# Where V of the second half and GpSimd's weight splits stand in a hybrid convolution, attention and expert kernel

## The chip, the core and the metric

The kernel runs on one core of one Trainium2 chip. Its time is the device time of one execution in microseconds. The engines of a core have queues of their own and meet through semaphores: TensorE (PE; its weight loads are PEld), VectorE (DVE), ScalarE (ACT), GpSimd (POOL), and SyncE (SP), which issues most DMAs.

## What is computed

`x` is 4 x 128 x 16 x 16, float32: 1024 tokens of 128 channels. Its three parts follow each other, and each adds to its input.

```python
# 1: convolutional attention over rows; q, k have 16 channels, v 128
x = gamma * einsum('bchk,bhwkv->bcwv', v, softmax(energy)) + x
# 2: tokens t (B, 256, 128), 8 heads of 16
n = layernorm(t)
k, q, v = n @ Wk, n @ Wq, n @ Wv
scores = einsum('bnhd,bmhd->bnmh', k, q) / sqrt(16)
t = t + softmax(scores, axis=-2) @ v
# 3: 8 experts, hidden size 512, the best two by gate logits
n = layernorm(t)
comb = softmax(top 2 of n @ gate_w.T), 0 for the other experts
for e in range(8):
    out += comb[:, e] * (gelu(n @ w1[e].T + b1[e]) @ w2[e].T + b2[e])
t = t + out
```

The reference normalizes each part's tokens as `(n - mean) / sqrt(var + 1e-5)`.

## The kernel before, in words

Channels lie on the partitions, tokens along them. The 1024 tokens are two halves of 512 (four images of 256). The first half goes through convolution and attention; then the expert loop runs over both halves, and the attention of the second half is laid between its steps.

**The expert loop** has 64 steps `n` (`STEPS`): 4 steps of 128 hidden rows for each of 8 experts, for each half (a visit is one expert on one half). `up(n)` makes 128 hidden rows from three passes: w1 and x are each split into a high part and a rest (`w1h`, `w1l`, `x2h`, `x2l`). ScalarE's `gelu(n)` writes `G`. From step 12 on (`SPLIT`, without steps 18 and 22) `G` is also split: a cast makes `Gh` (`high_gelu`, VectorE up to step 23, then ScalarE), a subtraction on VectorE makes `Gl` (`low_gelu`). `down(n)` multiplies with w2, in three passes with `w2h`, `w2l` where `G` is split and in one float32 matmul (two passes in the trace) where it isn't. `LAGS` says how many steps a down-projection lags: at step 12 downs 8, 9 and 10 are issued, at step 16 downs 11 to 14. `weigh(k)` (VectorE) scales a finished visit, `accumulate(k)` (GpSimd) adds it to the output: the first at about step 9, the second at 13.

**w2's split.** ScalarE copies `w2h` of experts 3, 4, 5, 6, 7, 0, 1, 2 (`W2_ORDER`) behind the GELUs of steps 0 to 7. GpSimd's `low_weights2` subtracts to get `w2l`, in the same order, at the places of its own in-order queue that `LOW_W2` gives. GpSimd's queue also holds the gate's exponential (`gate_exp`, at step 2), the pair sums of probabilities (`pair`, at steps 11, 15, 19, 23) and the accumulates. At one step the order is `gate_exp`, `pair`, `low_weights2`, `accumulate`.

**The gate of the first half** runs on VectorE at steps 0 to 4: `top_logits`, `top_experts` (ends with the gap subtraction `g_gap`), GpSimd's `gate_exp`, and `top_weights`, five small operations, each waiting for an earlier one, between the raw maxima (`raw_max`, L682) of steps 2 and 3. TensorE's raw scores (`raw_heads`, L1031) wait for the raw maximum before them.

**The attention of the second half.** Raw scores at steps 2 to 9, `max_transpose` at step 10 and `max_rows` on VectorE, which `scores_of_four(u)` waits for. Units `u` of four heads follow at steps 11, 15, 19 and 23 (`SCORES`): TensorE's scores into banks 4 to 7, two exponentials on ScalarE (`exps`, L503; banks 4 and 5, then 6 and 7), two pair sums on GpSimd. Exponential and GELU need different tables, so each unit has two table loads. On ScalarE `exps` stand ahead of `gelu` of the same step. At step 16 TensorE issues `sums` and `values` of units 4 and 5, behind the downs. V of the second half is projected by `project_v(1)` and copied out by `values_out(1)` (ScalarE, behind the GELU of step `VALUES_AT`).

Of the kernel before, what the change touches and what calls it, by code (L numbers as in the profile page):

```python
# [23 lines left out]
NHALF = T // HALF  # L24
# [14 lines left out]
W2_ORDER = [3, 4, 5, 6, 7, 0, 1, 2]  # L39
# [3 lines left out]
def hybrid_program(nc, x_in, xk_in, convw, convb, bv, gamma, attw, gate, w1, w2, b1, b2, consts, out):  # L43
# [5 lines left out]
    with ExitStack() as ctx:  # L49
# [3 lines left out]
        def sem(name):  # L53
            return ctx.enter_context(nc.semaphore(name))
# [115 lines left out]
        v_done, v_ready, vzero = sem("v_done"), sem("v_ready"), sem("vzero")  # L170
        raw_done, max_ready = sem("raw_done"), sem("max_ready")
        nmT_done, nmT_ready = sem("nmT_done"), sem("nmT_ready")
        score_done, prob_ready, paired, pv_done = sem("score_done"), sem("prob_ready"), sem("paired"), sem("pv_done")
# [13 lines left out]
        part_ready, acc_done, out_sent = sem("part_ready"), sem("acc_done"), sem("out_sent")  # L187
# [27 lines left out]

        FIRST_KQ, SECOND_KQ = (6, 7, 5, 1), ((0, 0), (0, TOK), (1, 0), (1, TOK))
        KQ_BANK = (4, 5, 6, 7)
        V_BANK = [0, 2]
        WARM_BANK = [3, 4, 0, 1]
        U_BANK, Y_BANK, GATE_BANK = (0, 1), (2, 3), (3, 4)  # L220

# [3 lines left out]
        GATING = [0, 32]  # L225
        RAW0, RAW_STEPS, NORM = 2, 8, 27
        SCORES, ATTENDS = {11: 4, 15: 5, 19: 6, 23: 7}, {16: 2, 24: 3}
        LATE_SCORES = (19,)
        HEADS_AT = {0: (2, 3)}
        VALUES_AT = 10  # L230

        G_LOGITS, G_ORDER, G_EXP, G_WEIGHTS, G_ROWS = 0, 1, 2, 2, 4

        SPLIT0, ACT_HIGH = 3 * MT, 24
        SPLIT = [n for n in range(SPLIT0, STEPS) if n not in (18, 22)]
        HIGH_W2 = {n: e for n, e in enumerate(W2_ORDER)}
        LOW_W2 = {n + 1: e for n, e in enumerate(W2_ORDER)}

        def high_engine(n):
            return "dve" if n < ACT_HIGH else "act"  # L240

        def high_count(n):
            return sum(high_engine(k) == high_engine(n) for k in SPLIT if k <= n)

        def split_count(n):
            return sum(k <= n for k in SPLIT)

        def downs(n):

            return range(max(0, n - LAGS[n - 1]) if n else 0, n + 1 - LAGS[n])  # L250

        def part_of(tiles, g, rows, c):

            p = c.start // HALF
            return tiles[p][g][rows, c.start - p * HALF:c.stop - p * HALF]
# [11 lines left out]
        def raw_slot(n):  # L267

            r = n - RAW0
            return (TILES + r // 2, r % 2) if 0 <= r < RAW_STEPS else None  # L270
# [51 lines left out]
        def _(pool):  # L322
# [19 lines left out]
            def low_weights2(e):  # L342

                pool.wait_ge(w2h_ready, W2_ORDER.index(e) + 1)
                if e == W2_ORDER[0]:
                    pool.wait_ge(pv_done, 4)
                    pool.wait_ge(sums_done, 4)
                nc.gpsimd.tensor_tensor(w2l[e][:, :], w2_sb[:, e, :], w2h[e][:, :].bitcast(f32), ALU.subtract)\  # L348
                    .then_inc(w2l_ready, 1)

            def pair(u, s):

                j = slice(2 * s, 2 * s + 2)
                pool.wait_ge(prob_ready, 2 * u + s + 1)
                if u >= 2:
                    pool.wait_ge(sums_done, u - 1)
                nc.gpsimd.tensor_tensor(pairs[:, u % 2, j, :], probs_of(u)[:, j, 0, :], probs_of(u)[:, j, 1, :],  # L357
                                        ALU.add).then_inc(paired, 1)
# [37 lines left out]
            for n in range(STEPS):  # L396
# [5 lines left out]
                if n in SCORES:  # L402
                    for s in range(2):
                        pair(SCORES[n], s)
                if n in LOW_W2:
                    low_weights2(LOW_W2[n])
                for k in range(VISITS - 2):
# [5 lines left out]
        def _(act):  # L413
# [67 lines left out]
            def other_heads(n):  # L481
                act.wait_ge(qkv_done, 8 + n + 1)
                heads_out(n, PS[:, KQ_BANK[n], :], cols(1))

            def values_out(p):

                act.wait_ge(v_done, p + 1)
                act.wait_ge(vzero, 2 * (p + 1))
                dst = vpad[p][:, :, :, :].rearrange("p t h c -> p (t h c)")\
                    .rearrange("p (th r) -> p th r", r=64)  # L490
                src = PS[:, V_BANK[p], :].rearrange("p (th r) -> p th r", r=32)
                for par in range(2):
                    nc.scalar.activation(dst[:, :, 48 * par:48 * par + DK], src[:, :, DK * par:DK * (par + 1)], ACT.Copy)\
                        .then_inc(v_ready, 1)
# [63 lines left out]
            for n in range(STEPS):  # L558
# [4 lines left out]
                for h in HEADS_AT.get(n, ()):  # L563
                    other_heads(h)
                if n == VALUES_AT:
                    values_out(1)
# [282 lines left out]
        def _(pe):  # L849
# [137 lines left out]

            def project_v(p):
                if p:
                    pe.wait_ge(part_ready, 1)  # L990
                else:
                    pe.wait_ge(act_kq_ready, 4)
                for t in range(TILES):
                    last = mm(PS[:, V_BANK[p], t * 128:(t + 1) * 128],
                              xn[:, p * HALF + t * 128:p * HALF + (t + 1) * 128],
                              attw_sb[:, 512:640], start=True, stop=True)
                last.then_inc(v_done, 1)

            def head_rows(j):
                return slice(32 * j, 32 * j + 32)  # L1000
# [77 lines left out]
            def scores_of_four(u):  # L1078

                b, g = u // 2, u % 2  # L1080
                pe.wait_ge(nmT_ready, 6)
                pe.wait_ge(prob_ready, 2 * u)
                if u == 6:
                    pe.wait_ge(t2_ready, 3)
                tok = slice(b * TOK, (b + 1) * TOK)
                for mt in range(2):
                    m = slice(b * TOK + mt * 128, b * TOK + (mt + 1) * 128)
                    for j in range(4):
                        last = mm(PS[:, 4 + j, mt * TOK:(mt + 1) * TOK], part_of(qT, g, head_rows(j), m),
                                  part_of(kT, g, head_rows(j), tok), start=True, stop=True)  # L1090
                        if mt and j % 2:
                            last.then_inc(score_done, 1)
# [72 lines left out]
            def down(n):  # L1165

                k, m = n // MT, n % MT
                e = k % E
                if m == 0:
                    if k in (0, E // 2):  # L1170
                        pe.wait_ge(w2_in[k // (E // 2)], 16)
                    if k >= 2:
                        pe.wait_ge(part_ready, k - 1)
                    if k == 1:
                        pe.wait_ge(combT_ready, 1)
                    if k == 2:
                        pe.wait_ge(v_ready, 2 * NHALF)
                y, ms = PS[:, Y_BANK[k % 2], :], slice(m * 128, (m + 1) * 128)
                if n not in SPLIT:
                    pe.wait_ge(gelu_done, n + 1)  # L1180
                    mm(y, w2_sb[:, e, ms], G[:, n % GR, :], start=(m == 0), stop=(m == MT - 1)).then_inc(down_done, 1)  # L1181
                    return
                if m == 0:
                    pe.wait_ge(w2l_ready, W2_ORDER.index(e) + 1)
                pe.wait_ge(g_high[high_engine(n)], high_count(n))
                mm(y, w2h[e][:, ms], Gh[:, n % GR, :], start=(m == 0), stop=False)  # L1186
                mm(y, w2l[e][:, ms], Gh[:, n % GR, :], start=False, stop=False)  # L1187
                pe.wait_ge(g_low, split_count(n))
                mm(y, w2h[e][:, ms], Gl[:, n % GR, :], start=False, stop=(m == MT - 1)).then_inc(down_done, 1)  # L1189
# [68 lines left out]
            for n in range(STEPS):  # L1258
                if raw_slot(n):
                    raw_heads(*raw_slot(n))  # L1260
                if n in SCORES and n not in LATE_SCORES:
                    scores_of_four(SCORES[n])
                up(n)
                if n in LATE_SCORES:
                    scores_of_four(SCORES[n])
                if n == RAW0 + RAW_STEPS:
                    max_transpose()
                for h in HEADS_AT.get(n, ()):
                    project_other(h)
                if n == VALUES_AT:  # L1270
                    project_v(1)
                for p in range(NHALF):
                    g = n - GATING[p]
                    if g == G_LOGITS:
                        logits(p)
                    if g == G_ROWS:
                        comb_rows(p)
                if n == NORM:
                    norm_center(5)
                if n == NORM + 1:  # L1280
                    norm_var(5)
                for d in downs(n):
                    down(d)
                if n in ATTENDS:
                    for u in (2 * ATTENDS[n], 2 * ATTENDS[n] + 1):
                        sums(u)
                        values(u)
                if n == NORM + 2:
                    norm_spread(5)
            for n in range(STEPS - LAGS[-1], STEPS):  # L1290
                down(n)
# [46 lines left out]
```

## Time and profile before

| | |
|---|---|
| median of 3 runs (lowest, highest) | 186.39 us (186.04, 187.66) |
| the profiled execution: its own time | 186.13 us |
| its span | 184.2 us |
| busy: PE, PEld | 174.1 us (95%), 118.6 us (64%) |
| busy: DVE, ACT, POOL | 117.1 us (64%), 123.2 us (67%), 79.5 us (43%) |
| granted TensorE clock | 1.0 throughout |

The span runs from the first to the last instruction of the profiled execution; its own time includes what lies around the span. Busy times are of that one execution. A line of the timeline gives the start, the duration, the engine, the line of the kernel, what was written from what, how many instructions were merged, and in brackets how long the engine was idle before and what released it. A merged line's duration is that of all its instructions.

### The profile page before, as it was taken

The numbers are of one execution on the slowest core, as the hardware profiler recorded it, in microseconds if no ns is written. First come the engines' busy times: TensorE is split into PE (matmuls) and PEld (weight loads), VectorE is DVE, ScalarE is ACT, GpSimd is POOL, SyncE is SP. The second block draws the span as 40 slices with busy tenths as digits, with TensorE's granted clock in tenths as the row PEclk, the third lists the DMA queues.
The fourth block names the chain that finished last, engine by engine and source line by source line (L and its number), as shares of the span: only waits on it lengthen the run. The fifth ranks groups of instructions, "written<-read, shape, count | busy, mean of one in ns | idle before, by whom it ended". The sixth has DMA issues, their size and how long they took to land.

```text
span 184.2 us, 3336 instructions
## 1 busy us (share of the span) xinstructions
PE 174.1 (95%) x1277; PEld 118.6 (64%) x1277; DVE 117.1 (64%) x199; ACT 123.2 (67%) x185; POOL 79.5 (43%) x68
## 2 busy tenths in 40 slices
PE   6999999989898998999999999999999999999991
PEld 3267867665466544447466567567887888888880
DVE  1569544985465396456084959397888677676673
ACT  3516953317727743545988598867878999999970
POOL 8404228988703284452536093524151152333312
PEclk9999999999999999999999999999999999999999
DMA  5799200000000000570000000000000880000001
GB/s 141 276 374 419 96 0 0 4 0 4 0 5 0 2 0 4 181 271 7 0 0 5 0 0 0 4 0 0 0 7 4 244 269 0 0 4 0 0 0 57
DMA packets 5791, 10.94 MB, mean 59 GB/s; under 512 B 1280, under 2 KB 1664, under 8 KB 5520
## 3 DMA queue, kind: packets, MB, share of 16 engines
q1 hardware_dynamic: 5360, 10.65, 16.7%
q8 instruction: 10, 0.16, 0.3%
q10 hardware_dynamic: 416, 0.08, 0.3%
q14 instruction: 5, 0.04, 0.1%
HBM read 10.17 MB, written 0.56 MB: 58 GB/s over the span
## 4 chain that ended last, share of the span: by engine, by line
PE 73%; issue 8%; ACT 7%; POOL 4%; DVE 4%; DMA 2%; ACTq 0%; DVEq 0%; POOLq 0%
PE PS L1159 9%; PE PS L1163 7%; PE PS L1160 7%; PE PS L1186 6%; PE PS L1189 6%; PE PS L1187 6%; PE PS L1181 4%; POOL pairs L357 4%; PE PS L1017 3%; PE PS L1031 3%; ACT room L516 2%; PE PS L910 2%; PE PS L878 2%; PE PS L1104 2%; DMA convw_sb<-convw 2%
## 5 line engine op out<-in xcount | busy, mean ns | idle before, releaser
L516 ACT ACTIVATE room<-PS,b_sb 128x512 f32<-128x512 f32 x64 | 43.6, 688 | 22.6 <-PE PS L1163 21.2
L772 DVE TENSOR_TENSOR Gl<-room,Gh 128x512 fp32r<-128x512 f32 x50 | 41.2, 831 | 13.7 <-ACT Gh L461 13.0
L365 POOL TENSOR_TENSOR x_sb<-x_sb,room 128x512 f32<-128x512 f32 x15 | 23.6, 1572 | 56.0 <-DVE room L781 56.0
L1159 PE MATMUL PS<-x2h,w1h 128*128 128x512 f32 x64 | 27.4, 427 | 1.2 <-ACT room L516 0.8
L461 ACT ACTIVATE Gh<-room 128x512 fp32r<-128x512 f32 x40 | 25.3, 633 | 1.3
L1163 PE MATMUL PS<-x2l,w1h 128*128 128x512 f32 x64 | 25.5, 398 | 0.0
L1160 PE MATMUL PS<-x2h,w1l 128*128 128x512 f32 x64 | 25.2, 393 | 0.0
L1186 PE MATMUL PS<-Gh,w2h 128*128 128x512 f32 x50 | 20.8, 416 | 0.0
L1187 PE MATMUL PS<-Gh,w2l 128*128 128x512 f32 x50 | 19.8, 395 | 0.0
L1189 PE MATMUL PS<-Gl,w2h 128*128 128x512 f32 x50 | 19.7, 395 | 0.0
L1159 PEld LDWEIGHTS PS<-x2h,w1h 128*128 128x128 f32 x64 | 12.0, 187 | 10.6 <-issue 4.9
L348 POOL TENSOR_TENSOR w2l<-w_sb,w2h 128x512 fp32r<-128x512 f32 x8 | 10.2, 1279 | 12.6 <-ACT w2h L455 12.6
L357 POOL TENSOR_TENSOR pairs<-shared_probs 128x512 f32<-128x512 f32 x10 | 13.7, 1390 | 4.6 <-ACT shared_probs L503 4.6
L1163 PEld LDWEIGHTS PS<-x2l,w1h 128*128 128x128 f32 x64 | 12.0, 188 | 3.5 <-DVE x2l L718 0.6
L682 DVE TENSOR_REDUCE other_nmx<-PS 128x4 f32<-128x1024 f32 x8 | 9.8, 1224 | 6.7 <-PE PS L1031 6.7
L1181 PE MATMUL PS<-room,w_sb 128*128 128x512 f32 x28 | 14.0, 592 | 0.0
L1160 PEld LDWEIGHTS PS<-x2h,w1l 128*128 128x128 f32 x64 | 12.0, 188 | 2.0
L767 DVE CAST Gh<-room 128x512 fp32r<-128x512 f32 x10 | 4.4, 444 | 13.5 <-ACT room L516 13.5
L503 ACT ACTIVATE shared_probs<-PS 128x1024 f32<-128x1024 f32 x12 | 11.6, 1022 | 1.9 <-PE PS L1074 1.7
L781 DVE SCALAR_TENSOR_TENSOR room<-PS,b_sb,room 128x512 f32<-128x512 f32 x16 | 11.9, 744 | 0.7 <-PE PS L1189 0.7
L373 POOL TENSOR_TENSOR ny<-nv,half_power 128x2 f32<-128x2 f32 (+1 forms) x6 | 4.9, 811 | 15.1 <-DVE nv L651 14.4
L1187 PEld LDWEIGHTS PS<-Gh,w2l 128*128 128x128 f32 x50 | 9.4, 188 | 2.6 <-issue 0.5
(136 smaller groups left out, 294.2 us busy)
## 6 DMA issues: line engine op xcount, KB each, us to landing
room<-comb_rows SPq DMA_DIRECT2D x16, 256.0 KB, 5.2
w1raw<-w SPq DMA_DIRECT2D x8, 256.0 KB, 5.9
w_sb<-w SPq DMA_DIRECT2D x2, 1024.0 KB, 10.6
x_sb<-x SPq DMA_DIRECT2D x2, 256.0 KB, 3.2
dev<-xk SPq DMA_DIRECT2D x1, 512.0 KB, 6.3
out<-x_sb SPq DMA_DIRECT2D x2, 256.0 KB, 4.2
attw_sb<-attw SPq DMA_DIRECT2D x1, 320.0 KB, 6.8
cst<-consts SPq DMA_DIRECT2D x1, 228.5 KB, 6.5
```

The lines of the kernel that those rows point to most:

```text
L357: nc.gpsimd.tensor_tensor(pairs[:, u % 2, j, :], probs_of(u)[:, j, 0, :], probs_of(u)[:, j, 1, :], ALU.add).then_inc(paired, 1)
L365: nc.gpsimd.tensor_tensor(t2[:, cols(p)], t2[:, cols(p)], part[:, s, :], ALU.add).then_inc(acc_done, 1)
L461: nc.scalar.activation(Gh[:, n % GR, :], G[:, n % GR, :], ACT.Copy)\
L516: nc.scalar.activation(G[:, n % GR, :], PS[:, U_BANK[n % 2], :], ACT.Gelu, bias=b1_sb[:, c:c + 1])\
L772: nc.vector.tensor_tensor(Gl[:, n % GR, :], G[:, n % GR, :], Gh[:, n % GR, :].bitcast(f32), ALU.subtract)\
L1159: mm(o, w1h[e][:, ms], x2h[:, cols(p)], start=True, stop=False)
L1160: mm(o, w1l[e][:, ms], x2h[:, cols(p)], start=False, stop=False)
L1163: mm(o, w1h[e][:, ms], x2l[:, cols(p)], start=False, stop=True).then_inc(up_done, 1)
L1181: mm(y, w2_sb[:, e, ms], G[:, n % GR, :], start=(m == 0), stop=(m == MT - 1)).then_inc(down_done, 1)
L1186: mm(y, w2h[e][:, ms], Gh[:, n % GR, :], start=(m == 0), stop=False)
L1187: mm(y, w2l[e][:, ms], Gh[:, n % GR, :], start=False, stop=False)
L1189: mm(y, w2h[e][:, ms], Gl[:, n % GR, :], start=False, stop=(m == MT - 1)).then_inc(down_done, 1)
```

## The change

V of the second half is projected at step 12, behind its three downs, into bank 6, and no longer at step 10 into bank 2; it waits for the tenth count of `prob_ready` (both exponentials of unit 4) instead of the first weighing. ScalarE's copies follow GELU 12. The wait for these copies moves from the first down-projection of visit 2 to the scores of unit 5. The up-projection of step 11 is issued ahead of the scores of unit 4 (`LATE_SCORES`). GpSimd's splits of w2 stand at steps 5 to 12 of its queue in place of 1 to 8: behind `gate_exp`, and those of experts 0, 1, 2 behind the first accumulate (step 9), of 1 and 2 also behind the pair sums of unit 4 (step 11).

```diff
-        V_BANK = [0, 2]
+        V_BANK = [0, 6]
...
-        LATE_SCORES = (19,)
+        LATE_SCORES = (11, 19)
         HEADS_AT = {0: (2, 3)}
-        VALUES_AT = 10
+        VALUES_AT = 12
...
-        LOW_W2 = {n + 1: e for n, e in enumerate(W2_ORDER)}
+        LOW_W2 = {n + 5: e for n, e in enumerate(W2_ORDER)}
...
             def project_v(p):
                 if p:
-                    pe.wait_ge(part_ready, 1)
+                    pe.wait_ge(prob_ready, 10)
...
                 pe.wait_ge(nmT_ready, 6)
                 pe.wait_ge(prob_ready, 2 * u)
+                if u == 5:
+                    pe.wait_ge(v_ready, 2 * NHALF)
...
                     if k == 1:
                         pe.wait_ge(combT_ready, 1)
-                    if k == 2:
-                        pe.wait_ge(v_ready, 2 * NHALF)
...
-                if n == VALUES_AT:
-                    project_v(1)
                 for p in range(NHALF):
...
                 for d in downs(n):
                     down(d)
+                if n == VALUES_AT:
+                    project_v(1)
```

## Rows read from the trace of the kernel before

**Rows 1.** The page: the chain by engine (part 4), two groups of VectorE (part 5).

```profile
PE 73%; issue 8%; ACT 7%; POOL 4%; DVE 4%; DMA 2%; ACTq 0%; DVEq 0%; POOLq 0%
...
L767 DVE CAST Gh<-room 128x512 fp32r<-128x512 f32 x10 | 4.4, 444 | 13.5 <-ACT room L516 13.5
...
L781 DVE SCALAR_TENSOR_TENSOR room<-PS,b_sb,room 128x512 f32<-128x512 f32 x16 | 11.9, 744 | 0.7 <-PE PS L1189 0.7
```

**Rows 2.** Timeline of PE and one weight load, 85 to 100 us.

```profile
85.31 1.06 PE L994 MATMUL PS<-attw_sb,xn 128*128 128x128 f32 x8
86.41 1.15 PE L1089 MATMUL PS<-other_kT,other_qT 32*128 32x256 f32 x16
86.41 0.74 PEld L1089 LDWEIGHTS PS<-other_kT,other_qT 32*128 32x128 f32 x16 [0.24 <-DVE other_kT L695]
87.49 0.50 PE L1159 MATMUL PS<-x2h,w1h 128*128 128x512 f32 x1
...
88.98 2.74 PE L1181 MATMUL PS<-room,w_sb 128*128 128x512 f32 x6
92.36 0.50 PE L1159 MATMUL PS<-x2h,w1h 128*128 128x512 f32 x1 [0.64 <-ACT room L516]
...
93.95 1.15 PE L1089 MATMUL PS<-other_kT,other_qT 32*128 32x256 f32 x16
...
99.24 0.40 PE L1189 MATMUL PS<-Gl,w2h 128*128 128x512 f32 x1
```

**Rows 3.** Timeline of ACT, 83 to 95 us.

```profile
83.94 1.38 ACT L516 ACTIVATE room<-PS,b_sb 128x512 f32<-128x512 f32 x2 [1.71 <-PE PS L1163]
86.40 0.66 ACT L493 ACTIVATE other_vpad<-PS 128x256 f32<-128x256 f32 x2 [1.08 <-PE PS L994]
...
88.37 1.94 ACT L503 ACTIVATE shared_probs<-PS 128x1024 f32<-128x1024 f32 x2
90.33 1.28 ACT L516 ACT_TABLE_LOAD   x1
91.62 1.27 ACT L516 ACTIVATE room<-PS,b_sb 128x512 f32<-128x512 f32 x2
93.36 1.39 ACT L516 ACTIVATE room<-PS,b_sb 128x512 f32<-128x512 f32 x2 [0.47 <-PE PS L1163]
```

**Rows 4.** Timelines of POOL, DVE and PE, 63 to 70 us.

```profile
63.37 1.27 POOL L348 TENSOR_TENSOR w2l<-w_sb,w2h 128x512 fp32r<-128x512 f32 x1 [5.60 <-ACT w2h L455]
64.74 1.01 POOL L378 TENSOR_TENSOR g_exp<-euler,g_gap 128x4 f32<-128x4 f32 x1
...
67.35 1.28 POOL L348 TENSOR_TENSOR w2l<-w_sb,w2h 128x512 fp32r<-128x512 f32 x1 [0.36 <-ACT w2h L455]
...
64.00 0.66 DVE L736 TENSOR_TENSOR g_gap<-g_top 128x4 f32<-128x4 f32 x1
...
66.34 0.67 DVE L746 TENSOR_SCALAR g_sum<-g_exp 128x4 f32<-128x4 f32 x1
...
67.42 1.25 DVE L752 TENSOR_TENSOR comb<-g_oh,g_rcp 128x32 f32<-128x32 f32 x1
...
69.87 0.71 PE L1031 MATMUL PS<-other_qT,other_kT 32*128 32x256 f32 x8 [0.58 <-DVE other_nmx L682]
```

**Rows 5.** Timelines of POOL and DVE, 89 to 99 us.

```profile
89.47 2.48 POOL L357 TENSOR_TENSOR pairs<-shared_probs 128x512 f32<-128x512 f32 x2 [3.16 <-ACT shared_probs L503]
94.81 1.41 POOL L365 TENSOR_TENSOR x_sb<-x_sb,room 128x512 f32<-128x512 f32 x1 [2.86 <-DVE room L781]
...
95.10 1.67 DVE L772 TENSOR_TENSOR Gl<-room,Gh 128x512 fp32r<-128x512 f32 x1
...
97.16 1.84 POOL L357 TENSOR_TENSOR pairs<-shared_probs 128x512 f32<-128x512 f32 x1 [0.94 <-ACT shared_probs L503]
```

**Rows 6.** Timelines of POOL and DVE, 123 to 126 us.

```profile
123.32 1.67 POOL L365 TENSOR_TENSOR x_sb<-x_sb,room 128x512 f32<-128x512 f32 x1 [5.80 <-DVE room L781]
...
123.76 1.78 DVE L772 TENSOR_TENSOR Gl<-room,Gh 128x512 fp32r<-128x512 f32 x1
```

## The prediction

> **What bounds the kernel now.** I read the page first, then the timeline of the two stretches that the edits touch, engine by engine. The page's chain [rows 1] gives TensorE 73% of the span and "issue" 8%; TensorE is busy 95% of it. So a time moves only if a TensorE gap closes or opens, and there are two small gaps where the diff works. The first stands at 69.87 us: TensorE is idle 0.58 us ahead of the raw scores of step 4, released by VectorE's raw maximum of step 3 [rows 4]. The second stands at 92.36: 0.64 us ahead of the up-projection of step 13, released by the GELU of step 11 [rows 2]. The reader should see in the ScalarE rows [rows 3] why that GELU is late: GELU of step 10 ends at 85.32, ScalarE waits 1.08 for V, copies V out (0.66), loads the exp table, runs two exponentials (88.37, 1.94 together), loads the GELU table (1.28), and only then computes GELU 11 at 91.62. After the gap everything on TensorE is a chain, each up-projection waiting for a GELU two steps back, so a shift at step 17 is a shift of the end.
>
> **Part 1, V behind the downs of step 12, up-projection 11 ahead of the scores.** Nothing is added: V is the same 8 matmul passes, the same two copies. What moves, on the old time scale:
> The scores of unit 4 still wait for the max rows, whose release came at 86.41 [rows 2] (its weight-load row). Before, V (85.31, 1.06 long) filled the time up to it. Now up-projection 11 does: two ups take 93.95 - 92.36 = 1.59, one 0.80, so 85.31 to 86.11, hidden. Scores start at 86.41 as before.
> The scores end at 86.41 + 1.15 = 87.56. ScalarE started its copy 0.03 after V's end (85.31 + 1.06 = 86.37, then 86.40), so the exponentials can start at 87.59. The table load has no V to wait for: from 85.34 to 86.62, over in time. Before they started at 88.37, so ScalarE gains 0.78. Then exponentials 1.96, table 1.28: GELU 11 starts at 90.84 (91.62 before), its result is there at 91.55, GELU 12 ends at 92.11.
> TensorE: up-projection 12 now stands at 87.49 and takes 0.80: 88.29. Before, two ups stood there, to 88.98. Downs 8, 9, 10 (six passes) took 2.74, less an overlap of about 0.05: 90.98. V costs 0.99 without its overlapped end: 91.97. So up-projection 13 starts at 91.97, not at 92.36: **0.39 gained**, of the 0.64 gap and the 0.78 on ScalarE, because V now lies on TensorE's path where it used to be free. If the cover at 85.31 to 86.41 were not filled, nothing more would be lost, since the scores wait anyway.
> The new waits: V waits for the tenth exponential result (about 89.6), long past. Scores 5, and all that TensorE has queued behind, wait for V's copies: these run after GELU 12, 92.14 to 92.80, and scores 5 come at 93.95 - 0.39 = 93.56. No cost; a slack of 0.76. GELU 13 follows up-projection 13 by 1.00 (92.36 to 93.36), so at 92.97, after the copies. All of the next unit is 0.39 earlier: GELU 14 ends at 94.36, the table is in at 95.64, exponentials 5 start at 95.66.
> The Trainium skill (ScalarE: Activation LUTs, section What ACT_TABLE_LOAD costs) states a drain of about 1.38 us on top of a load of 1.283, for every change of set. In the rows here a load takes 1.28 and the next activation starts 0.01 later (90.33 + 1.28 = 91.61, then 91.62) [rows 3]; by the Trainium skill's sum the load from 85.34 would hold the exponentials to 88.00, and 0.41 of ScalarE's 0.78 would be gone, which still leaves V's end as the last wait. The measurement decides.
>
> **Part 2, GpSimd's splits.** A split is 1.27 to 1.28 us of subtraction over two SBUF inputs, eight of them. GpSimd's queue is in order and not tied to TensorE's steps, so a plan "four steps later" only changes what the splits stand before and after. Three things change: the gate's exponential comes ahead of the first split; splits 0, 1, 2 come behind the first accumulate, which waits for VectorE's weighing at about 85; and splits 1 and 2 come behind the pair sums of unit 4. The down-projections need no split earlier than that of expert 3, at about 96, so no data is late.
> What is late is VectorE. The rows show that a VectorE operation with SBUF inputs doesn't run beside such a GpSimd operation: the gap subtraction on 4 elements took 0.66, from 64.00 to 64.66, against the split of 63.37 to 64.64, and the last gate multiply on 32 elements 1.25, to 68.67, against the split from 67.35 to 68.63 [rows 4]. Gl beside an accumulate (94.81 + 1.41 = 96.22) took 1.67, to 96.77: it finishes 0.55 after the other lets go. And GpSimd waits for VectorE too: a pair sum of 1.24 took 1.84 when Gl had begun first [rows 5].
> Who goes first when both wait? The second Gl at 123.76 was issued behind another Gl and 0.44 after the accumulate of 123.32, and it took 1.78: the accumulate, which had waited, got in between, ended at 124.99, and Gl at 125.54 [rows 6]. So they take turns by order of issue.
>
> *The gate, 64 to 70 us.* The subtraction is no longer held: no row shows it alone, and I take 0.17, between nothing and the 0.44 of a cast on 512 elements [rows 1]; so the gate's exponential starts near 64.25, not 64.74, and ends near 65.26. Then the three first splits, whose inputs are there, follow without a gap: to 66.5, 67.8 and 69.05. VectorE comes out of the first raw maximum at 66.34 with five dependent small operations, four of them on SBUF. Before, the pause of GpSimd up to 67.35 let four of them through and only the last was held. Now the first gets its turn at 66.5, the next (or the next two) at 67.8, the next after 69.05; the last ends at 69.05 + 0.1 to 69.05 + 0.3, against 68.67. Raw maximum and raw scores follow directly. **Cost 0.4 to 0.7, I take 0.6**, nearer to three separate turns, since each operation waits for the one before. The TensorE gap at 69.87 grows from 0.58 to about 1.2. The other end is a gain: if VectorE's small operations all pass, the gap closes, -0.58. Steps 4 to 10 have no slack on TensorE that would take the shift back.
>
> *The splits behind unit 4, 89 to 100 us* (old scale, without that shift). Pair sums started 1.10 after the exponentials (89.47 against 88.37), and two took 2.48: now 88.69 to 91.17. Splits 1 and 2 follow: to 92.44, and to 93.7, or 93.95 if the cast of GELU 12 (issued 92.14, waiting) has its turn between. Gl 12 then ends at 93.95 + 0.55 = 94.5. The weighing, which read PSUM, goes on: 0.74 [rows 1], to 95.15. The accumulate follows at about 95.2 and holds until 96.6 (its 1.41). The cast of GELU 13 lies beside its start (0.44, rows 1). Gl 13 ends at 96.6 + 0.55 = 97.15. Before, it ended at 96.77. Meanwhile exponentials 5 are 0.39 early, so their first pair sum is ready at 95.66 + 1.10 = 96.76, not at 97.16. That is the point: before, the cast and Gl of step 14 were both issued ahead of the pair sum, whose 1.84 shows that it waited for Gl [rows 5]. Now the pair sum is issued at 96.76 and the cast at 97.07. By turns: pair sum to 98.4, cast to 98.7, second pair sum to 99.9, Gl 14 to 100.45. TensorE wants Gl 14 for the last pass of step 14's down-projection at 99.24 - 0.39 = 98.85 [rows 2] and gets it at 100.5. **Cost 1.65, so the stretch ends 1.26 later than before**, the 0.39 of part 1 spent. Sums, attention and step 17 stand behind it on TensorE in one queue. Bounds: if the cast goes first and the pair sum second, Gl 14 ends near 99.3, a stall of 0.45, net nothing; if both go first, net -0.39. I take 1.26 because the issue times are 0.3 apart (0.1 if the cast has no turn between the splits). Here the Trainium skill (SBUF — State Buffer, section Who interferes with whom) says that the operation issued first has the shared ports for its whole length; the row of the second Gl agrees.
>
> **Sum.** 186.13 (the profiled run; span 184.2 and 1.93 around it) + 0.6 + 1.26 = **188.0**. The profiled run lies 0.26 below the median of 186.39.
>
> **Rivals.**
> B: only the gate is late, and step 14's cast slips in before the pair sum. Speaks for it: the margin is 0.1 to 0.35, and a shift of this size in either chain turns it. 186.13 + 0.6 + (0 to -0.39) = 186.3 to 186.7.
> C, the other side, faster: VectorE is held at neither place. The mechanism lies at 66.5: if GpSimd's next split doesn't take the ports as soon as the last one ends, the small gate operations pass in one run, as the four before 67.35 did. It decides once the last gate multiply ends before 68.1, from where the gap of 0.58 is gone, -0.58. With the undisturbed -0.39 of V: 186.13 - 0.97 = 185.2. Against it: the multiply of 67.42 lost to a split by 0.07 already.
> D: the gate costs nothing or gains, the splits behind unit 4 stall step 14: 186.13 + 1.26 + (0 to -0.58) = 186.8 to 187.4.
> E: the change doesn't do what it says, since V on TensorE's path and Gl's delays cancel its gain and the gate comes out level: 186.1.
>
> **How the numbers follow.** Chances: forecast 0.42, B 0.26, C 0.12, D 0.14, E 0.06. The range runs from 185.3 (most of C) to 188.7 (the upper bound of the gate term, 0.7, and some 0.6 of spread between runs). A measurement of this kernel can tell about 1% from no change: that is 184.5 and 188.3 around the median. The forecast lies just inside, so a third to a half of it, and nothing of the rest, is slower by over 1%: 0.20. Faster by over 1% needs more than C gives: 0.03.
>
> **What would show it.** Part 1: up-projection 11 between the max transposes and the scores; GELU 11 some 0.8 earlier after the max rows; no TensorE idle ahead of up-projection 13. Gate: three splits in a row, the last gate multiply's end right after the third, and over 1 us idle ahead of the next raw scores. Unit 4: two splits directly behind two pair sums, Gl 12 over 1 us long, a cast of step 14 over 1 us long, and TensorE idle, released by Gl, ahead of the last pass of step 14. The prediction is wrong if the second is absent (then B or C), or if that Gl is 0.69 long.

## The result, and the profile after

The changed kernel takes 187.57 us (median of 14 runs, 187.45 to 190.89) where the kernel before takes 186.20 (14 runs, 185.98 to 189.05): ratio 1.0082, 95% interval 1.006 to 1.0104. It is 1.37 us slower; 188.0 had been forecast. The highest values of every series here are executions with a lower granted TensorE clock (in the profile of e5 it was 0.83 in the first 20 us and 1.00 after them); a median called "at full clock" below is that of the executions with a mean granted clock of 0.994 or more, and the profiles whose rows are shown have 0.996 or more. The profiled execution after took 187.58, its span is 185.6 against 184.2.

The page after: the chain and the cast, as in [rows 1], the two groups of TensorE that now have idle time ahead of them, and GpSimd's splits:

```profile
PE 70%; issue 9%; DVE 9%; ACT 6%; POOL 4%; ACTq 0%; DVEq 0%; POOLq 0%
...
L1186 PE MATMUL PS<-Gh,w2h 128*128 128x512 f32 x50 | 20.9, 418 | 0.3 <-DVE Gh L767 0.3
L1189 PE MATMUL PS<-Gl,w2h 128*128 128x512 f32 x50 | 19.8, 397 | 1.0 <-DVE Gl L772 1.0
...
L767 DVE CAST Gh<-room 128x512 fp32r<-128x512 f32 x10 | 5.6, 559 | 10.4 <-ACT room L516 10.4
L348 POOL TENSOR_TENSOR w2l<-w_sb,w2h 128x512 fp32r<-128x512 f32 x8 | 10.3, 1302 | 2.9 <-ACT w2h L455 2.9
```

VectorE's share of the chain has gone from 4% to 9%, its mean cast from 444 ns to 559, and TensorE's passes over `Gh` and `Gl` have idle time ahead of them that VectorE releases. No work was added: busy TensorE time is 174.4 us against 174.1.

**The gate.** Timelines after of DVE, POOL (each of the first three splits by itself) and PE, 63 to 71 us, against [rows 4]:

```profile
63.94 0.17 DVE L736 TENSOR_TENSOR g_gap<-g_top 128x4 f32<-128x4 f32 x1
66.27 0.20 DVE L746 TENSOR_SCALAR g_sum<-g_exp 128x4 f32<-128x4 f32 x1
66.38 0.18 DVE L747 TENSOR_TENSOR g_oh<-g_oh,g_exp 128x32 f32<-128x32 f32 x1
66.59 0.18 DVE L749 RECIPROCAL g_rcp<-g_sum 128x4 f32<-128x4 f32 x1
66.69 1.05 DVE L750 TENSOR_TENSOR g_oh<-g_oh 128x32 f32<-128x32 f32 x1
67.78 1.21 DVE L752 TENSOR_TENSOR comb<-g_oh,g_rcp 128x32 f32<-128x32 f32 x1
...
65.16 1.28 POOL L348 TENSOR_TENSOR w2l<-w_sb,w2h 128x512 fp32r<-128x512 f32 x1
66.40 1.30 POOL L348 TENSOR_TENSOR w2l<-w_sb,w2h 128x512 fp32r<-128x512 f32 x1
67.65 1.28 POOL L348 TENSOR_TENSOR w2l<-w_sb,w2h 128x512 fp32r<-128x512 f32 x1
...
70.17 0.71 PE L1031 MATMUL PS<-other_qT,other_kT 32*128 32x256 f32 x8 [0.95 <-DVE other_nmx L682]
```

And one row of the kernel before that [rows 4] lacks, the split between the gate's exponential and the one of 67.35 (timeline, POOL):

```profile
65.71 1.27 POOL L348 TENSOR_TENSOR w2l<-w_sb,w2h 128x512 fp32r<-128x512 f32 x1
```

The gap subtraction takes 0.17, the value I had taken. The splits follow without a pause. Before, two of the five small operations were held: the first (66.34, 0.67 long, to 67.01) until the split of 65.71 was over at 66.98, and the last (1.25). After, the first loses almost nothing (0.20), and two others are held: the fourth (1.05) until the second split is over at 67.70, the fifth (1.21) until the third is, at 68.93. The chain of five takes 2.72 from its first start to its last end, where it took 2.33: 0.39 more. The gap ahead of the raw scores grows from 0.58 to 0.95, so the gate costs 0.37.

**Unit 4.** The timelines after, 85 to 101 us: PE against [rows 2], ACT against [rows 3], POOL and DVE against [rows 5].

```profile
86.73 1.15 PE L1091 MATMUL PS<-other_kT,other_qT 32*128 32x256 f32 x16 [0.24 <-DVE other_kT L695]
88.61 2.73 PE L1181 MATMUL PS<-room,w_sb 128*128 128x512 f32 x6
91.19 1.05 PE L994 MATMUL PS<-attw_sb,xn 128*128 128x128 f32 x8
92.00 0.48 PE L1161 MATMUL PS<-x2h,w1h 128*128 128x512 f32 x1
...
96.15 1.02 PE L1181 MATMUL PS<-room,w_sb 128*128 128x512 f32 x2
98.89 0.50 PE L1186 MATMUL PS<-Gh,w2h 128*128 128x512 f32 x1 [0.33 <-DVE Gh L767]
100.58 0.50 PE L1189 MATMUL PS<-Gl,w2h 128*128 128x512 f32 x1 [0.96 <-DVE Gl L772]
101.00 0.64 PE L1123 MATMUL PS<-pairs,cst 128*32 128x256 f32 x8
...
85.66 1.28 ACT L503 ACT_TABLE_LOAD   x1
87.91 1.94 ACT L503 ACTIVATE shared_probs<-PS 128x1024 f32<-128x1024 f32 x2 [0.97 <-PE PS L1091]
...
91.46 2.70 POOL L348 TENSOR_TENSOR w2l<-w_sb,w2h 128x512 fp32r<-128x512 f32 x2
95.45 1.40 POOL L365 TENSOR_TENSOR x_sb<-x_sb,room 128x512 f32<-128x512 f32 x1 [1.29 <-DVE room L781]
96.81 1.75 POOL L357 TENSOR_TENSOR pairs<-shared_probs 128x512 f32<-128x512 f32 x1
...
93.06 1.65 DVE L772 TENSOR_TENSOR Gl<-room,Gh 128x512 fp32r<-128x512 f32 x1
95.74 1.66 DVE L772 TENSOR_TENSOR Gl<-room,Gh 128x512 fp32r<-128x512 f32 x1
97.32 1.52 DVE L767 CAST Gh<-room 128x512 fp32r<-128x512 f32 x1
98.87 1.65 DVE L772 TENSOR_TENSOR Gl<-room,Gh 128x512 fp32r<-128x512 f32 x1
```

To set the sizes, four more rows of the kernel before (timelines, DVE and PE): the cast and Gl of step 14, the start of step 16's downs and that of the sums behind them:

```profile
96.69 0.42 DVE L767 CAST Gh<-room 128x512 fp32r<-128x512 f32 x1
97.14 0.69 DVE L772 TENSOR_TENSOR Gl<-room,Gh 128x512 fp32r<-128x512 f32 x1
...
96.52 1.02 PE L1181 MATMUL PS<-room,w_sb 128*128 128x512 f32 x2
...
99.56 0.64 PE L1121 MATMUL PS<-pairs,cst 128*32 128x256 f32 x8
```

Before, Gl of step 14 was issued (the start that the timeline gives) at 97.14, 0.02 ahead of the first pair sum of unit 5 (97.16, [rows 5]), and lasted 0.69. After, the pair sum is issued at 96.81, 0.51 ahead of the cast (97.32).

Measured from the scores of unit 4 (86.41 before, 86.73 after), up-projection 13 starts after 5.27 us where it took 5.95, and the downs of step 16 after 9.42 where it was 10.11: 0.69 gained. There is no gap ahead of up-projection 13. The exponentials no longer wait for a table load but for the scores (0.97). From the downs of step 16 to the sums it is 101.00 - 96.15 = 4.85, against 3.04: 1.81 lost. The page's idle figures, 0.33 and 0.96, show only 1.29 of it, for two reasons: a pass that follows an idle stretch has 0.34 to the next start instead of 0.23, and the idle time counts from a modelled end (0.39 after the start) where the next pass would have started after 0.23. The reader should take starts, not idle columns, to size a stall on TensorE.

Together: -0.69 + 1.81 = 1.12 behind the scores. At the gate it is 0.39, since the scores of unit 4 stand 0.32 later though the loop began 0.07 earlier (its first up-projection at 59.19, before 59.26). So 1.12 + 0.39 - 0.07 = 1.44, which is the distance of the two sums (101.00 - 99.56), and the spans differ by 1.4.

### The profile page after: what moved, and what is told of

The parts are those of the page before. It is cut to its first block, busy times and chain, and to the rows that moved or that the text cites. A ratio compares the mean times of both kernels' runs of the same rounds, so it can differ in the third digit from the quotient of the medians.

```text
span 185.6 us, 3336 instructions
## 1 busy us (share of the span) xinstructions
PE 174.4 (94%) x1277; PEld 118.4 (64%) x1277; DVE 120.1 (65%) x199; ACT 123.1 (66%) x185; POOL 79.5 (43%) x68
## 4 chain that ended last, share of the span: by engine, by line
PE 70%; issue 9%; DVE 9%; ACT 6%; POOL 4%; ACTq 0%; DVEq 0%; POOLq 0%
PE PS L1161 8%; PE PS L1165 7%; PE PS L1162 6%; PE PS L1189 6%; PE PS L1186 5%; PE PS L1187 5%; POOL pairs L357 4%; PE PS L1181 3%; PE PS L855 3%; ACT room L516 3%; PE PS L1017 3%; PE PS L1031 2%; PE PS L910 2%; PE PS L878 2%; PE PS L1106 2%
## 5 line engine op out<-in xcount | busy, mean ns | idle before, releaser
L772 DVE TENSOR_TENSOR Gl<-room,Gh 128x512 fp32r<-128x512 f32 x50 | 43.2, 871 | 13.6 <-ACT Gh L461 13.0
L1181 PE MATMUL PS<-room,w_sb 128*128 128x512 f32 x28 | 14.0, 592 | 0.0
L767 DVE CAST Gh<-room 128x512 fp32r<-128x512 f32 x10 | 5.6, 559 | 10.4 <-ACT room L516 10.4
L1189 PEld LDWEIGHTS PS<-Gl,w2h 128*128 128x128 f32 x50 | 9.4, 188 | 3.6 <-DVE Gl L772 1.4
L1186 PEld LDWEIGHTS PS<-Gh,w2h 128*128 128x128 f32 x50 | 9.4, 188 | 3.2 <-DVE Gh L767 0.8
```

The costliest lines, as they stand in the source:

```text
L772: nc.vector.tensor_tensor(Gl[:, n % GR, :], G[:, n % GR, :], Gh[:, n % GR, :].bitcast(f32), ALU.subtract)\
```

## The experiments

All were timed in 5 rounds beside the kernel before (186.10 to 186.25 in these series); intervals are of the ratio to it.

**e1, the splits back.** The changed kernel with one line undone.

```diff
-        LOW_W2 = {n + 5: e for n, e in enumerate(W2_ORDER)}
+        LOW_W2 = {n + 1: e for n, e in enumerate(W2_ORDER)}
```

> The changed kernel with the splits of w2 back at steps 1 to 8 (V and the up-projection of step 11 stay as changed). Theory (the loss is made by GpSimd's splits alone): the gap ahead of the raw scores of step 4 is 0.58 again, the cast and Gl of step 14 are issued ahead of the pair sums of unit 5 and last 0.4 and 0.7, and what is left is part 1's gain. In the trace after, up-projection 13 stood 0.67 us earlier behind the max rows than before, so 186.2 - 0.67 = 185.5. Rival (part 1 itself brings the pair sum ahead of the cast, since the exponentials of unit 5 come earlier): Gl of step 14 is still over 1.5 us long and the time is near 186.5 or above.

185.47 us (185.40 at full clock), ratio 0.996 (0.9923 to 0.9997). Timelines of DVE and POOL:

```profile
95.89 0.41 DVE L767 CAST Gh<-room 128x512 fp32r<-128x512 f32 x1
96.34 0.69 DVE L772 TENSOR_TENSOR Gl<-room,Gh 128x512 fp32r<-128x512 f32 x1
...
96.45 2.98 POOL L357 TENSOR_TENSOR pairs<-shared_probs 128x512 f32<-128x512 f32 x2 [1.03 <-ACT shared_probs L503]
```

Cast and Gl of step 14 are both issued ahead of the pair sum, Gl by 0.11, although the exponentials come as early as in the changed kernel. Part 1 is a gain of 0.7 by itself (at full clock 185.40 against 186.06 for the kernel before), and the whole loss is the splits'.

**e2, the splits alone.** The opposite half: the kernel before, with `LOW_W2` at `n + 5`.

> The kernel before with only the splits moved to steps 5 to 12. Theory: the gate costs 0.37 as after, and behind unit 4 the two splits run 0.8 us later than in the changed kernel, since the exponentials do; Gl 12 ends near 95.3 on the old scale, the accumulate near 97.4, the pair sum (ready at 97.16) goes ahead of the cast of step 14, and Gl 14 ends near 101.3 where TensorE wants it at 99.24: 2.05 lost, with the gate 2.4, so 188.6. Rival (the splits cost what they cost in the changed kernel, 0.37 + 1.29 of stalls): 187.9.

188.57 us (188.30 at full clock), ratio 1.0124 (1.008 to 1.0167). The gap ahead of the raw scores of step 4 is 0.94, and TensorE waits again ahead of both kinds of pass of step 14:

```profile
97.08 1.02 PE L1181 MATMUL PS<-room,w_sb 128*128 128x512 f32 x2
...
99.89 0.50 PE L1186 MATMUL PS<-Gh,w2h 128*128 128x512 f32 x1 [0.40 <-DVE Gh L767]
101.57 0.50 PE L1189 MATMUL PS<-Gl,w2h 128*128 128x512 f32 x1 [0.94 <-DVE Gl L772]
102.01 0.64 PE L1121 MATMUL PS<-pairs,cst 128*32 128x256 f32 x8
```

From the downs to the sums it is 102.01 - 97.08 = 4.93, which is 1.89 more than 3.04; the theory had 2.05 there. With the gate's 0.37 that makes 2.26, and the medians at full clock differ by 188.30 - 186.06 = 2.24: between the theory (2.4) and the rival (1.7), nearer to the theory. In the changed kernel the splits cost 187.54 - 185.40 = 2.14 at full clock.

**e3 and e4, the two places of the splits apart.** Both are the changed kernel. e3 puts the splits at steps 3 to 10, behind the gate's exponential but ahead of the pair sums of unit 4; e4 keeps the first five at 1 to 5 and the last three at 10 to 12.

```diff
-        LOW_W2 = {n + 5: e for n, e in enumerate(W2_ORDER)}
+        LOW_W2 = {n + 3: e for n, e in enumerate(W2_ORDER)}                        # e3
+        LOW_W2 = {n + (1 if n < 5 else 5): e for n, e in enumerate(W2_ORDER)}      # e4
```

> The changed kernel with the splits at steps 3 to 10: behind the gate's exponential as changed, but all ahead of the pair sums of unit 4. Theory: the gate's cost of 0.37 stays, the stall at step 14 is gone, so 186.2 + 0.37 - 0.67 = 185.9. Rival (the split behind the first accumulate, or part 1, makes the stall too): 187 or above.

> The changed kernel with the first five splits back at steps 1 to 5 and the last three at steps 10 to 12. Theory: no cost at the gate, the gap ahead of the raw scores of step 4 is 0.58 as before, the stall of step 14 (0.33 ahead of the second and 0.96 ahead of the last kind of pass) stays: 187.57 - 0.37 = 187.2. Rival (the gate's delay is absorbed later, so that taking it away brings nothing): 187.6.

e3: 185.96 us (185.81 at full clock), 0.9965 (0.9927 to 1.0002), the gap at the gate 0.95, no stall at step 14. e4: 187.29 us (187.27), 1.0036 (1.0003 to 1.0069), the gap 0.58, stalls of 0.33 and 0.95. So from e1, at full clock, the gate takes 0.41 and the two splits behind unit 4 take 1.87, near the 1.81 read above. Both came within 0.1 of the theory; the medians alone wouldn't settle the gate's size, the gap in the traces (0.95 against 0.58) does.

**e6, the pair sums made to wait.** The changed kernel; the first pair sum of unit 5 waits for Gl of step 14. Splits, Gl 12 and Gl 13 are as late as before.

```diff
                 pool.wait_ge(prob_ready, 2 * u + s + 1)
+                if u == 5 and s == 0:
+                    pool.wait_ge(g_low, split_count(14))
```

> The changed kernel, its splits as changed, but the first pair sum of unit 5 waits until Gl of step 14 is written. Theory (the stall is the turn of the pair sums between the cast and Gl of step 14): cast 14 and Gl 14 last 0.4 and 0.7, TensorE passes step 14 with no stall, but the pair sums now end near 101.3, 0.85 behind what the sums of unit 5 want: 1.29 given back, 0.85 lost less the part hidden, so the sums of unit 5 stand 0.97 earlier and the time is 187.57 - 0.97 = 186.6. Rival (the lateness comes from Gl 12 and Gl 13, held by the splits and the accumulate, whatever the pair sums do): cast 14 still starts near 97.3 and TensorE still waits for it over 0.5 us, and the time is 187.4 or above.

186.85 us (186.72 at full clock), 1.0046 (1.0021 to 1.0071). Timelines of DVE, POOL and PE:

```profile
97.48 0.41 DVE L769 CAST Gh<-room 128x512 fp32r<-128x512 f32 x1
97.93 0.69 DVE L774 TENSOR_TENSOR Gl<-room,Gh 128x512 fp32r<-128x512 f32 x1
...
98.76 2.70 POOL L359 TENSOR_TENSOR pairs<-shared_probs 128x512 f32<-128x512 f32 x2 [1.74 <-ACT shared_probs L505]
...
99.02 0.40 PE L1191 MATMUL PS<-Gl,w2h 128*128 128x512 f32 x1
101.60 0.64 PE L1125 MATMUL PS<-pairs,cst 128*32 128x256 f32 x8 [0.75 <-POOL pairs L359]
```

The cast starts at the same place (97.48, in a trace that runs 0.16 later) and lasts 0.41 in place of 1.52; the stall at step 14 is gone, and a smaller one stands ahead of the sums of unit 5. That separates the two readings: the lateness of Gl 12 and 13 only takes away the margin, the time is lost in the turns that the pair sums get. The pair sums end at 101.46, 101.3 once the 0.16 is taken off, as expected, and the sums of unit 5 start 0.88 earlier than in the changed kernel by the same reckoning (101.60 against 102.32), where 0.97 was expected. At full clock the medians differ by 187.54 - 186.72 = 0.82, near the 0.88 read here; what made this trace late by 0.16 from the loop's start on is open.

**e7 and e8, the two moves of part 1 apart.** e7: V at step 12, but up-projection 11 behind the scores, splits at 1 to 8. e8: the kernel before with `LATE_SCORES = (11, 19)` only.

```diff
-        LATE_SCORES = (11, 19)
+        LATE_SCORES = (19,)        # e7, on the changed kernel with the splits back
```

> V at step 12 in bank 6 as changed, but the up-projection of step 11 behind the scores again and the splits back at steps 1 to 8. Theory (the two moves of part 1 need each other): TensorE stands idle ahead of the scores for about 1.0 us, since V no longer fills the wait for the max rows; the downs start at 88.98 as before and V (0.81) follows at 91.56, so up-projection 13 starts near 92.37, as before: 186.2, no change. Rival (ScalarE's 0.78 earlier exponentials are the gain, whoever fills TensorE): 185.5.

> The kernel before with only the up-projection of step 11 ahead of the scores of unit 4. Theory: V and this up-projection both stand ahead of the scores, which start 0.8 later, at 87.2; the exponentials are bound by the table load that waits for V's copies (88.37) and by the scores (88.4), so nothing moves: 186.2. Rival (the later scores push the exponentials): up to 0.8 slower, 187.0.

e7: 186.21 us, 0.9992 (0.997 to 1.0014). e8: 186.34 us, 1.0017 (0.9995 to 1.0039). Neither move changes the time beyond the noise; together they are worth 0.7 (e1). In e7 ScalarE is as early as in e1, and TensorE loses it by idling (timeline of PE), the wait which V used to fill:

```profile
86.52 1.15 PE L1091 MATMUL PS<-other_kT,other_qT 32*128 32x256 f32 x16 [0.94 <-DVE other_kT L695]
```

In e8 V's copies stay on ScalarE's path, and the gap ahead of up-projection 13 is still there (0.76, at a granted clock of 0.991). e7 also has a turn lost by little: the cast of step 13, issued at 94.18, lasts 1.52 behind the accumulate issued at 94.15. It had the slack, so it cost nothing.

**e5, e9, e10, a version that beats both.** The changed kernel, splits at steps 3 to 10, and the first of them waits for the gate's last multiply. e9 is e5 again, for a second profile, whose rows are shown below. e10 is the same on the kernel before, without part 1.

```diff
-        LOW_W2 = {n + 5: e for n, e in enumerate(W2_ORDER)}
+        LOW_W2 = {n + 3: e for n, e in enumerate(W2_ORDER)}
...
                 if e == W2_ORDER[0]:
+                    pool.wait_ge(comb_ready, 1)
                     pool.wait_ge(pv_done, 4)
```

> The changed kernel with the splits at steps 3 to 10 and GpSimd's first split waiting for the gate's last multiply (comb_ready). Theory: VectorE's five small gate operations run in a row and end near 66.9, the raw maximum of step 3 starts with its raw scores at about 67.5, and TensorE's gap ahead of the raw scores of step 4 closes: 0.58 gained beside part 1's 0.67, so 186.2 - 1.25 = 184.95. Rival (something else bounds the raw scores of step 4, such as the splits now crowding later): the gap stays above 0.3 and the time is 185.3 or more.

> The kernel of e5 once more, for a profile of an undisturbed execution: TensorE's gap ahead of the raw scores of step 4 is gone or below 0.1, VectorE's last gate multiply lasts 0.2, and the time is 185.0 again. If the raw scores are still late by over 0.3, e5's gain has another cause.

> The kernel before with only GpSimd's splits changed: at steps 3 to 10, the first waiting for the gate's last multiply. If the two gains are independent (they lie on TensorE's queue 15 us apart, with no slack between): the gap of 0.58 closes and nothing else moves, 186.1 - 0.58 = 185.55. If part of it is taken back at the gap of 0.64 at 92.36 or the later splits crowd the first accumulate: 185.8 or more.

e5: 185.06 us (184.79 at full clock), 0.9949 (0.9922 to 0.9976). e9: 184.74 us (184.74), 0.9929 (0.991 to 0.9948). e10: 185.53 us (185.51), 0.998 (0.9954 to 1.0006). Timelines of e9, DVE, POOL and PE:

```profile
66.86 0.19 DVE L753 TENSOR_TENSOR comb<-g_oh,g_rcp 128x32 f32<-128x32 f32 x1
67.55 1.23 DVE L683 TENSOR_REDUCE other_nmx<-PS 128x4 f32<-128x1024 f32 x1 [0.49 <-PE PS L1032]
...
67.19 6.21 POOL L349 TENSOR_TENSOR w2l<-w_sb,w2h 128x512 fp32r<-128x512 f32 x5 [2.00 <-DVE comb L753]
...
69.16 0.71 PE L1032 MATMUL PS<-other_qT,other_kT 32*128 32x256 f32 x8
```

The last multiply lasts 0.19 in place of 1.21, VectorE waits for TensorE and no longer the other way, and the raw scores of step 4 start at 69.16 with nothing idle ahead (69.87 before, 70.17 after). The gate's gap was worth 0.7 in e10 and again 0.7 between e1 (185.40) and e9, more than the 0.58 of its idle time: by starts, the raw scores of step 4 come 0.95 behind the pass of L1181 ahead of them in both, 1.60 before. e3 and e9 have the splits at the same places and differ by the one wait: 1.07 at full clock. e9 is 1.5 us faster than the kernel before and 2.8 faster than the changed one. e5's median lies 0.3 above e9's for the same code; at full clock the two are 0.05 apart. e10's interval includes 1, so the median alone doesn't settle its gain; in its trace TensorE's gap is gone.

## Why the prediction was right

The forecast was the right case, and it came out 0.4 too high. Its steps:

- *Part 1 (forecast 0.39 gained, measured 0.69).* The mechanism held in each point: the scores wait for the max rows, the table load is over in time, V's copies delay nobody. The term was mis-sized in V's price on TensorE's path: I took 0.99, the timeline after has 92.00 - 91.19 = 0.81. And six passes cost 91.19 - 88.61 = 2.58, not 2.69. Both had been taken from durations less an overlap; start to start would have been right. One sentence of this part is wrong: "If the cover at 85.31 to 86.41 were not filled, nothing more would be lost". In e7 nothing fills it, up-projection 11 stands behind the scores, up-projection 13 starts 5.96 after the scores (5.95 before), and the whole gain is gone.
- *The table load.* ScalarE's load ran from 85.66 to 86.94 and the exponentials started at 87.91, when the scores were there (0.97 idle, released by TensorE). The GELU load of 89.87 is followed by its activation at 91.16, 0.01 after its 1.28. No drain beyond the load is visible, where the Trainium skill (ScalarE: Activation LUTs, section What ACT_TABLE_LOAD costs) states about 1.38 us for every change of set.
- *The gate (0.6, measured 0.37 to 0.39).* Two operations were held for long, not three, and the last ended at 68.99, 0.06 behind the third split, not 0.1 to 0.3. The step that failed is "the first gets its turn at 66.5, the next at 67.8". The second had been issued at 66.38, ahead of the split's 66.40, and went with the first; the reciprocal, issued at 66.59, ran beside the split. The fourth, issued at 66.69, was held. Order of issue had been my own rule; I hadn't followed it for operations 0.1 apart. That a reciprocal isn't held no row of before had shown. The prediction also misread the kernel before: "let four of them through and only the last was held" overlooks the first, held to 67.01. The sum doesn't change by it, as it goes by the end of the last. The sign "over 1 us idle ahead of the next raw scores" came out at 0.95; the other signs came as named.
- *The splits behind unit 4 (1.65, measured 1.81).* As forecast, operation by operation, each within 0.3 once the 0.32 by which unit 4 stands later is taken off: Gl 12 at 93.06 lasts 1.65, the pair sum is issued at 96.81, the cast at 97.32 lasts 1.52, Gl 14 ends at 100.52. e1, e4 and e6 show the cause: take away the two splits, or the pair sum's turn, and the stall goes. TensorE wanted Gl 14 0.30 earlier than forecast, by what part 1 gained more, but the chain on VectorE was earlier too, since the exponentials were: the last pass starts at 100.58 instead of 96.15 + 2.72 = 98.87, which is 1.71. The other 0.10 is the slower restart (0.42 from this pass to the sums, 0.32 before), which the forecast lacks.
- *The sum.* 0.39 + 1.81 - 0.69 = 1.51 by starts, less 0.07 of an earlier begin; measured 1.37 by the medians, forecast 1.86. The errors of the gate (0.21) and of part 1 (0.30) had the same sign, that of the stall (0.16) the other, so part of the closeness is that they cancel.

Of the rivals, C (the small operations pass in one run) is what e9 makes happen, and its price of 0.58 for the gate was near: 0.7. B needed the cast ahead of the pair sum; it came 0.51 behind, not the 0.3 of the forecast. Without the splits the order is close: in e1 Gl 14 is issued 0.11 ahead of the pair sum.

## What to carry to other kernels

An instruction moved within an in-order queue doesn't wait for its new place, only for what now stands ahead of it: here splits of an idle engine slid into the one microsecond in which another engine had a chain of five tiny operations, and two more delayed a cast and a subtraction of which the second had been issued only 0.02 ahead of a pair sum. When two engines exclude each other, write down the issue times on both around the move: with Gl issued 0.02 (before) or 0.11 (e1) ahead there was no stall, with the cast issued 0.51 behind TensorE lost 1.8. And hold bulk work behind the end of a short dependent chain, by one wait, rather than ahead of it by luck of timing.

## What the runs showed of the hardware

- Where both used SBUF, VectorE and GpSimd took turns by order of issue, to within 0.03 us: a cast issued 0.03 behind an accumulate lasted 1.52 (e7), a Gl issued 0.11 ahead of a pair sum 0.69 (e1) and one issued 0.02 ahead 0.69 too (before). Two operations issued ahead of the next GpSimd operation both went first: the gate's first two, at 66.27 and 66.38, the split at 66.40.
- A reciprocal on 128x4 float32 in SBUF ran beside a split (0.18; also 0.18 in e9, where no split runs), while a multiply of 128x32 issued 0.1 later was held for its whole rest (1.05).
- A TensorE pass behind an idle stretch held up the next by 0.34 (98.89 to 99.23) in place of 0.23, so the stalls cost more than the idle column shows: 1.81 against 1.29.
